# Low-rank products of a token mixer: two half products from a turned copy in place of four quarter products

## What is computed

```python
xxx = xa + sx * maa_x                                  # sx: the token before, minus this one
t = jnp.tanh(xxx @ maa_w1).reshape(B, L, 5, -1)        # 5 features of rank 32
m = jnp.einsum('blfd,fdc->blfc', t, maa_w2)            # 32 -> 256 channels, for each feature
mw, mk, mv, mr, mg = (m[:, :, j] for j in range(5))
xw = xa + sx * (maa_w + mw)                            # and so for k, v, r, g
```

## Time and profile before

| | |
|---|---|
| runs | 1144.70, 1146.26, 1146.98 us; median 1146.26 |
| profiled execution | 1145.66 us, span 1143.9 us |
| mean granted TensorE clock | 0.97 of full speed |
| TensorE, VectorE, ScalarE, GpSimd busy | 90%, 69%, 47%, 9% |
| instructions | 21369 |

### The profile page before, as it was taken

The page is one execution under the profiler, slowest core; times in us unless marked ns, Lnnn a source line. Parts: engine busy times, 40 slices in busy tenths (PEclk is TensorE's granted clock), DMA queues, the critical chain, the costliest instruction groups (busy, mean ns, idle before and its releaser), DMA issues.

```text
span 1143.9 us, 21369 instructions
## 1 busy us (share of the span) xinstructions
PE 1027.8 (90%) x8866; PEld 772.4 (68%) x8866; DVE 788.0 (69%) x1078; ACT 536.7 (47%) x1643; POOL 108.4 (9%) x101
## 2 busy tenths in 40 slices
PE   7747899989998899988999799998999979999998
PEld 5634567766776667755777577786667757787777
DVE  3698579866996679789964998748965589623320
ACT  1102236742655255632576256634664346625662
POOL 1001010101010010021200201010100100100000
PEclk9978999999999899998999999999999989999999
DMA  9200010000000000000000000001000000000000
GB/s 375 83 0 1 2 30 11 1 2 22 20 1 2 15 22 6 2 2 19 19 5 1 27 14 2 1 2 44 6 1 2 29 22 1 1 1 22 26 10 19
DMA packets 17058, 24.80 MB, mean 22 GB/s; under 512 B 4417, under 2 KB 13761, under 8 KB 16322
## 3 DMA queue, kind: packets, MB, share of 16 engines
q1 hardware_dynamic: 16962, 23.44, 6.1%
HBM read 17.13 MB, written 2.10 MB: 17 GB/s over the span
## 4 chain that ended last, share of the span: by engine, by line
PE 61%; DVE 21%; ACT 9%; issue 4%; POOL 2%; DMA 2%; SPq 1%; DVEq 0%; ACTq 0%; POOLq 0%
PE PA L1267 7%; PE PB L1301 6%; PE QB L1380 5%; DVE S_ L563 5%; PE PB L1129 5%; ACT big L1003 4%; PE QA L1129 4%; PE QA L1393 3%; PE PA L1184 3%; PE QA L1119 2%; PE PA L1119 2%; DVE A L571 2%; PE QA L1404 2%; PE QA L1088 2%; PE QB L1088 2%
## 5 line engine op out<-in xcount | busy, mean ns | idle before, releaser
L1003 ACT ACTIVATE big<-QB,nmax 128x128 f32<-128x128 f32 x512 | 181.0, 374 | 95.6 <-DVE nmax L659 95.3
L563 DVE TENSOR_TENSOR_SCAN S_<-W_,A 128x1024 f32<-128x1024 f32 x64 | 146.0, 2303 | 1.9 <-ACT A L857 1.7
L1301 PE MATMUL PB<-A,common_w 128*128 128x256 f32 x512 | 128.5, 395 | 17.3 <-DVE A L571 17.2
L1380 PE MATMUL QB<-big,QX 128*128 128x256 f32 x512 | 134.8, 386 | 10.2 <-DMA QX<-big 10.2
L659 DVE TENSOR_REDUCE nmax<-QB 128x4 f32<-128x512 f32 x128 | 86.5, 685 | 57.8 <-PE QB L1380 56.4
L1301 PEld LDWEIGHTS PB<-A,common_w 128*128 128x128 f32 x512 | 98.0, 198 | 38.4 <-DVE A L571 20.9
L1380 PEld LDWEIGHTS QB<-big,QX 128*128 128x128 f32 x512 | 99.4, 195 | 28.9 <-DMA QX<-big 11.6
L1267 PE MATMUL PA<-X,rwkv_w 128*32 128x128 f32 x3072 | 97.6, 283 | 17.2 <-DVE X L458 16.9
L1003 ACT ACTIVATION_READ_ACCUMULATOR big<-QB,nmax 128x1 f32 x512 | 109.7, 214 | 0.0
L1267 PEld LDWEIGHTS PA<-X,rwkv_w 128*32 128x32 f32 x3072 | 85.8, 114 | 31.0 <-DVE X L458 23.8
L449 DVE SCALAR_TENSOR_TENSOR PA<-PA,rwkv_w,SX 128x512 f32<-128x512 f32 x80 | 56.4, 751 | 61.2 <-PE PA L1184 55.4
(11 more groups left out here) (192 smaller groups left out, 1751.8 us busy)
## 6 DMA issues: line engine op xcount, KB each, us to landing
rwkv_w<-in_rwkv_w SPq DMA_DIRECT2D x2, 2866.0 KB, 14.5
QX<-big SPq DMA_DIRECT2D x128, 32.0 KB, 1.9
attn_w<-in_attn_w SPq DMA_DIRECT2D x2, 1031.5 KB, 16.8
mlp_w<-in_mlp_w SPq DMA_DIRECT2D x1, 2052.0 KB, 23.2
X<-in_x SPq DMA_DIRECT2D x4, 512.0 KB, 16.4
ctx<-in_ctx SPq DMA_DIRECT2D x4, 512.0 KB, 3.3
ctx<-in_ctx_t SPq DMA_DIRECT2D x4, 512.0 KB, 3.3
out<-XT SPq DMA_DIRECT2D x4, 256.0 KB, 2.0
```

The lines of the kernel that those rows point to most:

```text
L563: last = v.tensor_tensor_scan(S_[:, d].rearrange("p k t -> p (k t)"), W_[:].rearrange("p k t -> p (k t)"), A_[c % 2][:, d].rearrange("p k ...
L1003: last = s.activation(PR[:, n % 2, j], bank(2 + n % 2)[:, j * T:(j + 1) * T], ACT.Exp, bias=nmax[:, n % 2, j:j + 1], accum_out=den[:, b, h ...
L1301: last = t.matmul(y, ident, A_[c % 2][:, :, k], start=(c % 2 == 0 and k == 0), stop=False, skip_group_check=True)
L1380: last = t.matmul(o, QX[b % 2][:, i, h], K2[:, :, h, b * T:(b + 1) * T], start=False, stop=True, skip_group_check=True)
```

## The change

`maa` makes each feature by two matmuls of 512 tokens, one for each channel half, at once in two row tiles. They must read different rows, so channel half 1 reads a second tile, `low_turned`, which has the two 64-row halves of `low` exchanged. ScalarE makes it by two transfers on its own queue: it waits for its tanh to be written, issues both, and then takes the tanh of the fifth feature. TensorE waits for both transfers before the first feature. Since `low` now holds the same order of features for all tokens, the first product is one matmul over 512 tokens for each contraction half; `w1` has 5 blocks and `w2r` is gone, its channel half 1 standing in `w2a`. The step between the two pairs, with its wait, is gone, and the four strings of `ORDER` are written anew.

```diff
@@ RWKV_COLS, COUNTS @@
-RWKV_COLS = [("w1", HALF * 7 * MIX), ("w2a", C), ("w2r", C), ("w2b", C), ("dw1", HALF * DEC), ("dw2", C),
+RWKV_COLS = [("w1", HALF * NMIX * MIX), ("w2a", C), ("w2b", C), ("dw1", HALF * DEC), ("dw2", C),
...
@@ ScalarE, head @@
                     s.activation(low[:], PA[:, 0:512], ACT.Tanh).then_inc(sem["r_lowrank"], 1)
+                    act.wait_ge(sem["r_lowrank"], u.at("r_lowrank", 1))
+                    for h in range(2):
+                        act.dma_start(low_turned[64 * h:64 * h + 64], low[64 - 64 * h:128 - 64 * h]).then_inc(sem["r_low_moved"], 16)
                     s.activation(low5[:], PA[:, 512:512 + T], ACT.Tanh).then_inc(sem["r_lowrank"], 1)
@@ TensorE, maa @@
                         for h in range(HALF):
                             ready(h)
-                        for k in range(2):
-                            if k:
-                                yield
-                                pe.wait_ge(sem["r_pair"], u.at("r_pair", 2 * f + 2))
-                            for h in range(HALF):
-                                q = (h + k) % 2
-                                rows = MIX * ((f + 2 * q) % 4)
-                                w2 = r_(L, "w2r" if q else "w2a")[rows:rows + MIX, h * P:(h + 1) * P]
-                                last = t.matmul(pa(h)[:, 256 * q:256 * q + 256], w2, low[rows:rows + MIX, 256 * q:256 * q + 256],
-                                                start=True, stop=True, tile_position=(rows, 0))
-                                last.then_inc(sem["r_maa" if k else "r_pair"], 1)
+                        for h in range(HALF):
+                            rows = MIX * ((f + 2 * h) % 4)
+                            t.matmul(pa(h), r_(L, "w2a")[rows:rows + MIX, h * P:(h + 1) * P], (low_turned if h else low)[rows:rows + MIX],
+                                     start=True, stop=True, tile_position=(rows, 0)).then_inc(sem["r_maa"], 1)
@@ TensorE, head @@
-                        for q in range(2):
-                            t.matmul(PA[:, 256 * q:256 * q + 256], w1[:, h, 64 * q:64 * q + P], flat(X5[0])[:, h, 256 * q:256 * q + 256],
-                                     start=(h == 0 and q == 0), stop=(h == 1), skip_group_check=True)
+                        t.matmul(PA[:, 0:512], w1[:, h, 0:P], flat(X5[0])[:, h], start=(h == 0), stop=(h == 1))
...
-                    yield from maa(0, lambda h: pe.wait_ge(sem["r_lowrank"], u.at("r_lowrank", h + 1)))
+                    pe.wait_ge(sem["r_lowrank"], u.at("r_lowrank", 2))
+                    pe.wait_ge(sem["r_low_moved"], u.at("r_low_moved", 32))
+                    maa(0, lambda h: None)
...
-                        yield from maa(f, turned(f - 1))
+                        maa(f, turned(f - 1))
```

More of the change, by code:

```diff
@@ L56 @@
 COUNTS = {
-    "mixer": dict(r_stats=1, r_rstd=1, r_z=1, r_zT=2, r_xn=2, r_mixed=12, r_used=2, r_lowrank=2, r_pair=14, r_maa=10,
+    "mixer": dict(r_stats=1, r_rstd=1, r_z=1, r_zT=2, r_xn=2, r_mixed=12, r_used=2, r_lowrank=2, r_low_moved=32, r_pair=6, r_maa=10,
                   r_dec=1, r_decay=2, r_proj=6, r_wg=2, r_turned=8, r_w=1, r_tg=2, r_gate=1, r_rk=1, r_ru=1, r_out=1, r_vr=1, r_s0=4, r_rs=4,
@@ L105 @@
     "VectorE":
[L106 to L110, removed]
@@ L111 @@
-        "RARARAARARARRAARRAARRARAARRRAAHHARRRRHARHAHARRARRARAAHHRRRHAAAAAAAAAAAAAAAAAAHHHAAAAAAAHHHAAAAH",
+        "HHHHHHHHHHHHAHHRRHRRRRRHRRRRHRRRHRHRRHHRHHHRRRRHRRHAAAHHARRHAAHAAAARRRRAARRAAHHARRAARRRAHAARHAAAHRRR"
+        "AAAHHARRRRAARHAHHRRAAAAHHAAHHAAAHHARRAARRRRAARAARARARAHHARAARRRAAARRRHHAAHARHHARRARHHHRAAHRAHRAAAAHH"
+        "AAAAHHARRHAHARRRHHARAHAARHHAHRAARARHHRARRAARAAHHRRRAAARAHRHARRARRRARAHHAAARAAHHRRRRAAARARRRAARRRHHAR"
+        "AAHRRRAHHAARAHHRAARRARHHARRRAARRHHARAAAAAHHAARRRAAARRRAARRARRAARARRAARRRAHAHRAARHARHAAHHHRAARRRRAAHH"
@@ L112 @@
+        "RRRARAHHARHRHAAARHHRRRRRAAARRRAARAARAHARAHARRARAHAAHRAAAHRRRAAAHHRAARRRRAHAHAAARRRHHRRHHRHHRARARRAAA"
+        "RARARRAARARAARARRAARRARAARRRAAAHHRRRRAHRHARHARARRRAAARHHHRRAAAAAAAAAAAAAAAAAAHHHAAAAAAAHHHAAAAH",
     "GpSimd":
-        "HRRHAARRHAARRHAARHRARAHRRARRHRARAHRARARRHRAHAHHA",
+        "HRRHAARRHAARRHAARHRARAHRRRARHRARAHRARARRHRAHAHHA",
     "ScalarE":
-        "HHHHHHHHHHRHHRRRHRHRHRHHHHAHHAARAAHHAAAAAAAARAAAAAAAAHAAAAAAAARAAAHRAARARAHAARAAAAAAAHHHAHHAAAHHAHHR"
-        "AAAAAAAAAAAARAAAAAAAAAAAAAARAHRARHARAAHARAHAAARAHAAHAHHAAAAHHHHAAAAHAAAAAAHAAAARAAAAHAAAHAAHAAAARRAH"
@@ L117 @@
[L117 to L120, removed]
-    "TensorE":
[L122 to L130, removed]
@@ new lines @@
+        "HHHHHHHHHHHRHRRHHRRRHRHHHAHAHHAAAHHRAAAAAAAAAARAAAAHAAAAAARAAAAAAARHAARARAAAHAARAAAAAHHHAAHAHRAHHHHA"
+        "AAAAAAAAAAAAAAAAARAAARAAAAAAHARARHARAHAAARAAHAHAAAAHHHAAAAHHRHAHAAHAAAAAAAHAAARAAHAAAAHAHAAAAAARAAHH"
+        "AARRHARAAHAARAARHAAAAAHHAAARHAAAAAARAHAARAAAAHRAARAAAHAAAHRAAHAAAAHHRAAHAAHAARAAAAAAARARHHAAARAAAARA"
+        "AAAARAAAAAAAAHAAAAARAHARRAHARAAAHHAAAAAARHHHAARRHHARAAARHHAAAAAARAAAAAAAAAAAHAAAARAAAAAAAHRAARAARAHA"
+        "RAAAAAAAHHAHHHRARRHAAHRAAAAAHHRAAAAAAAAAARAAAAAAAAARAAAARAARARHARAAAAAAHAHRAAHRAARARAAHAAAAHHAAAAAAA"
@@ new lines @@
+        "AAAAAAAAAAAAAAAAHAHAHAAAAAAAAAAAHHAAAAAH",
+    "TensorE":
+        "HHHHHHHHHHHHHHHHHHHRRHRRHRRRRRRHRRRRHHRRRHHRHRHRHHAHAHHAHAAAHHAAAHAAAAHHARAAHRARAARAAHAARAHAAARRRARA"
+        "AAAAARRAAARAAHRARRRRAHAAAAHAARARAHAARHAHHAHHAAAHAAHHAHHHAAAAAAARHAAARAAARARAHAHAAHAAAHARRRAAARRAARRR"
+        "AHARAAAARRRRHAAHHAAAHRAAHHARAHAARAHHHAAAAAAHHHAHHAHHHHAAHHAAAAAAAAHAARRARRHAAHAAARHRAAAHAHRARAAAHRRR"
+        "AAAHAAARRRRRRHAHAAAAHAARHRARAAAHAHAHHHHHAAAAARRRRHHAAARRRAAARRARAARHARRAAAARRRHHRAAAHAAAHAAAHARHAAAA"
+        "RRAAHHRAHAAARHHAAHAAAAARRAAAARRAHHAAAAAAARRARARARAAHARAHHRAHRAARRAAARAHAAHAARAARRAARRHARAAAHHARAHRRH"
+        "AAHAAAHRAAHHAHARRAHHRAHRARAAHHAAAAAAAAHHRHAARRHRAAAARRAARAAHAAAHAAAARAAAAARRRAARHAAAARRRRRAAAHHAAARA"
+        "HRAAAAHARHAHAAAHHRAHRHRRHRHRAAHAAAHAAAAAAAARRAARAAAAAARRARAARHHRAAAAAHRAHRRAARARAARRRRHAAAHRAARAARAH"
+        "AHHARHHARAHHARAARRRAAAAHAAAHAHAHHAAHAAAAAAAAAAAAAAAAAAAAHAAAAAAHHHAHHHAAAAAAHAAAAHHAHHHAAAAAAHAH",
@@ L219, in build @@
         low = sb("low", [N])
+        low_turned = sb("low_turned", [N])
         low5 = sb("low5", [T])
@@ L1193, in maa_last @@
                                 yield
-                                pe.wait_ge(sem["r_pair"], u.at("r_pair", 8 + 2 * k))
+                                pe.wait_ge(sem["r_pair"], u.at("r_pair", 2 * k))
                             for h in range(HALF):
@@ L1227, in head @@
                         for q in range(4):
-                            last = t.matmul(PA[MIX * q:MIX * q + MIX, 512:512 + T], w1[:, h, 6 * MIX:7 * MIX],
+                            last = t.matmul(PA[MIX * q:MIX * q + MIX, 512:512 + T], w1[:, h, 4 * MIX:5 * MIX],
                                             flat(X5[0])[:, h, T * q:T * q + T], start=(h == 0), stop=(h == 1), tile_position=(0, MIX * q))
@@ L1512, in rwkv_pack @@
         w = lambda n: a[f"{pre}_{n}"]
-        w1 = w("maa_w1").reshape(C, NMIX, MIX)[:, [order[f] for f in (0, 1, 2, 3, 0, 1, 4)]].reshape(C, 7 * MIX)
+        w1 = w("maa_w1").reshape(C, NMIX, MIX)[:, order].reshape(C, NMIX * MIX)
         w2 = w("maa_w2")[order]
@@ L1516, in rwkv_pack @@
         return pack(RWKV_COLS, dict(
-            w1=mat(w1), w2a=w2[0:4].reshape(P, C), w2r=w2[[2, 3, 0, 1]].reshape(P, C),
+            w1=mat(w1), w2a=np.concatenate([w2[0:4].reshape(P, C)[:, 0:P], w2[[2, 3, 0, 1]].reshape(P, C)[:, P:C]], 1),
             w2b=np.tile(w2[4], (P // MIX, 1)), dw1=mat(w("decay_w1")), dw2=rows(dw2),
```

## The result

The changed kernel is slower: **1161.12 us** median of four runs (1157.54 to 1164.35) against 1146.62 (1144.70 to 1147.32), a ratio of **1.013 (95%: 1.0116 to 1.0143)**, 14.9 us. I had forecast 1144.7, in 1138 to 1151. The profiled execution of the changed kernel took 1159.89 us around a span of 1158.0.

A forecast was written before the change was run, and what follows sets the result against it. It took TensorE, busy 90% of the span and 61% of the chain, to bound the kernel. Terms -9.3 + 3.0 + 3.8 + 0.9 = -1.6 us gave 1144.7 us against the median of 1146.26, range 1138 to 1151.

The forecast's parts named there:

- a: Products of four features on TensorE: joining two pairs of matmuls into one removes 10.0 us, before weighting.
- b: First low-rank product on TensorE: two matmuls of 512 columns for four of 256 save 0.9 us, before weighting.
- e: ScalarE's queue: wait and two issues delay attention's exponentials and copies, +0.9 us (0 to 9).
- c: Unit 0: the first product of four features waits for the turned copy, +3.0 us; other bound 12.8 late.
- d: Units 1 to 7: TensorE's wait for the copies, partly covered by the new order, +3.8 us (0 to 16.8).
- Rival 4: Products on TensorE: joining saves only the waits, 3.3 us for 9.3, ending at 1150.7; chance 0.05.
- Rival 2: Unit 0: copies stand behind SP's blocked load issues, product 8.6 us late, ending at 1150.3; chance 0.15.
- Rival 3: Units 1 to 7: ScalarE's issues stop the exponentials, 9.0 us for 0.9, ending at 1152.8; chance 0.06.

The follow-up runs named there:

- e4: Changed kernel without the copies and their waits, in the order strings of before, half the mixing using wrong values: ratio 0.9929 to the kernel before.
- e3: Changed kernel without the copies and their waits, in the new order strings, half the mixing using wrong values: ratio 0.9982 to the kernel before.
- e6: Changed kernel, new order, copies issued but unread, TensorE waiting for them only at the second feature: ratio 1.0044 to the kernel before.
- e5: Changed kernel with copies and their wait in unit 0 alone, other units reading one tile: ratio 1.0111 to the kernel before.
- e11: As e6 (copies issued, unread, waited for only at the second feature), with the order strings of before: ratio 1.0021 to the kernel before.
- e8: Changed kernel, copies and waits included, with the order strings of before: ratio 1.0240 to the kernel before.
- e1: Changed kernel, but SP issues the inputs of groups 2 and 3 only after unit 0's copies have landed: ratio 1.0125 to the kernel before.
- e7: Changed kernel, with second-layer and MLP weights and later inputs issued only after unit 0's copies have landed: ratio 1.0045 to the kernel before.
- e2: Kernel before with its own products and no copy, in the new order strings: ratio 1.0050 to the kernel before.
- e12: As e4, plus two unread ScalarE Copy instructions of 64 rows behind both tanhs, no transfer: ratio 0.9988 to the kernel before.

## Why the prediction was wrong

| term | predicted, us | measured, us | from |
|---|---|---|---|
| a, b: joined products | -9.3 | -8.1 | e4 |
| the order itself | none | +6.1 | e3 - e4 |
| e: ScalarE's queue | +0.9 | +7.1 | e6 - e3 |
| c: unit 0's wait | +3.0 | +9.9 with d | changed kernel - e6 |
| d: units 1 to 7 | +3.8 | 2.3 of waits | waits of the changed kernel |
| sum | -1.6 | +14.9 | result |

Each ratio carries some 0.15% (1.7 us), so the differences are good to about 2.4 us. The sum closes because each term starts where the one before it ends; that confirms none of them. The measured terms depend on the order in which the parts are added: unit 0's copies alone, added to e3, cost 14.8 (e5), and by the old order the same 14.9 is -8.1 (e4), +10.5 (e11), +25.1 (e8) and -12.6 for the new order.

**a and b were right.** 0.21 us fixed and 0.21 for each 128 columns from two rows gave 1.06 us for a length that no row had, and the product at 47.54 holds 1.06. The first low-rank product holds TensorE 1.88 in unit 0 of the changed kernel (15.68 to 17.56), as b said. The total of 8.1 is my 10.9 at 0.74 rather than 0.85, and its interval holds both. Rival 4, no saving but the waits, falls with it.

From the 60 cycles that the Trainium skill, "TensorEngine Tiling (Array Packing)", Instruction Overhead, gives each matmul, I had estimated 4.6 us for a, with b 5.5 at most; the runs do not bear that estimate out. e4 shows at least 6.3, and a joined product holds TensorE 1.06 us where two pairs of before hold 1.28: 0.22 less, where the estimate has 0.05.

**c was wrong, and it is the largest step that failed.** "256 KB at that rate is 0.6 us more" priced the bytes of the copies at the engines' rate. The loads beside them made their packets run 5.45 us instead of 1.4 and start 2.6 us later: 10.4 us from tanh to product where I said 4.0, then half the clock. Rival 2 had the place, the sign and nearly the price (8.6 late at 28.1; it was 28.68), and its mechanism was wrong: e1 takes away every blocked issue of SP and nothing moves. The copies of the earlier trace rows, which I took as the nearest rows, ran beside idle engines; in e7, with idle engines, the product starts at 22.19, where my sum without the loads gave 21.96.

**d held its bounds, but it left out a cost.** The waits are half of what I counted (2.3 us against 4.5, 3.8 weighted); without the new cover they are 18.3, where my bound was 16.8. What I left out is the other side of it: "the new order string puts more work of the other programs there" counted only what the moved steps cover. The new order costs 6 by itself (e3 against e4, e2 against before). That the moved steps had covered something else at their old places would explain it; no trace here puts it in one place.

**e was wrong by its weight.** ScalarE's share of the chain, 9%, was taken for the part of added time that reaches the end; it is about 70% (e6, 7.1 of 10.2 us; e12, 6.8 of 10.1), each give or take some 2 us. Rival 3, 9.0 us with chance 0.06, was near: 7.1. One spot shows its mechanism at work, unit 3 in the timeline above: an issue pair of 1.98 us, and a value step before which TensorE stood 2.33 us. Once unit 0 is late, less of it is seen: the copies of units 1 to 7 add 2.2 us to e5, their waits with them.

The range failed because it took one rival at a time. The bounds of c and e (12.8 and 9) held the differences in the table, though not e5's 14.8; but the place of rival 2 and the mechanism of rival 3 came together, with a third cost, the order, that had no term.

## What to carry to other kernels

A small transfer beside a large one was priced here by packets, not bytes: its packets for each engine, times the packet time of the other queue, and a late first packet on top. ScalarE was half idle and 9% of the chain, and time put on it was not cheap; ask what stands behind it at that place, or add the same time there and measure. And when work is moved to cover a wait, measure the new order without the wait as well: it has a price of its own.

## What was not expected of the hardware

- A copy inside SBUF from ScalarE's queue lands in 2.2 to 3.3 us, mostly 2.3, in units 1 to 7 of the changed kernel, and in 7.4 and 9.1 us (7.5 and 9.1 with SP silent) under the loads (DMA share 0.91 to 1.05).
- The granted clock went to half within a wait of 9.4 us, and also around one of 3.7 us; the first product after each then takes 1.19 us a record instead of 0.66.
- ScalarE writes the tanh of rows 64 to 127 to rows 0 to 63 and the reverse, out of PSUM, at 0.59 us for 64 x 512, the time of 128 x 512 (0.60): an exchange of halves needs no transfer.
- An issue on ScalarE's queue takes 0.47 to 0.65 us of the engine where nothing is in its way (e6), and up to 1.47 (changed kernel, unit 3).
